# A new order of the first pair's front stages in a fused adapter-to-attention kernel

## The reference

```python
x = relu(x + df(x) * dt)                                   # L0: finite differences of x times five fixed grids
h = gelu(x @ down_W.T + down_b)                            # L1: adapter, 256 -> 64, with an expert per sequence
x = layernorm(x + (h @ expert_W[id].T + ...) @ up_W.T + up_b)
s, t = cond(time)                                          # L2: scale and shift from a small net on the time
y = silu(s * norm2d(x) + t) @ W_in + b_in                  #     norm2d: mean and variance over the whole 256 x 256
x = x + silu(s * norm2d(y) + t) @ W_out + b_out
x = ln(x) * (1 + scale) + shift                            # L3: scale and shift from a second embedding
q, k, v = x @ Wq + bq, x @ Wk + bk, x @ Wv + bv            #     16 heads of width 16
x = x + softmax(q k / 4 + attention_bias, masked) v @ Wo + bo
return x + (gelu2(ln(x) * g2 + beta2 @ W1 + b1) @ W2 + b2)
```

## Time and profile before

| what | value |
|---|---|
| median of three runs | 933.13 us (932.63 to 935.77) |
| span of the profiled execution | 929.6 us |
| median less that span | 3.5 us |
| PE busy | 856.0 us (92%) |
| DVE, ACT, POOL busy | 742.4, 727.5, 237.6 us |
| first product of q with k on record | at 92.17 us |

### The profile page before, as it was taken

One profiled execution on the slowest core, in us unless ns is written; L12 is line 12 of the kernel. 1 busy time (PEld: TensorE's weight loads), 2 busy tenths in 40 slices (PEclk: granted clock), 3 DMA queues, 4 the chain that ended last, 5 costly groups with the idle time before them and its releaser, 6 DMA issues.

```text
span 929.6 us, 18071 instructions
## 1 busy us (share of the span) xinstructions
PE 856.0 (92%) x5630; PEld 659.5 (71%) x5715; DVE 742.4 (80%) x2377; ACT 727.5 (78%) x1897; POOL 237.6 (26%) x236
## 2 busy tenths in 40 slices
PE   7775878999999999999999999999999999999987
PEld 6454656777777777777777777777777777777766
DVE  8556888898898898898898898898897898866542
ACT  1122978979898888979898888979898888988763
POOL 2232123224123323223123323223123323120000
PEclk9777899999999999999999999999999999999999
DMA  9813644554447363654447363554447363555400
GB/s 258 250 50 101 188 136 138 154 162 138 132 131 187 98 168 105 168 160 136 133 131 188 98 170 104 169 161 132 136 131 188 98 170 102 158 161 167 140 12 23
DMA packets 133081, 130.88 MB, mean 141 GB/s; under 512 B 18265, under 2 KB 123481, under 8 KB 132969
## 3 DMA queue, kind: packets, MB, share of 16 engines
q1 hardware_dynamic: 101616, 112.02, 42.9%
q10 hardware_dynamic: 31370, 17.71, 6.9%
HBM read 112.61 MB, written 17.07 MB: 140 GB/s over the span
## 4 chain that ended last, share of the span: by engine, by line
PE 58%; ACT 19%; DVE 7%; issue 3%; POOL 0%; ACTq 0%; DVEq 0%
PE ff_ps L1340 11%; PE ff_ps L1321 8%; PE PT_ps L1376 8%; ACT Pr L1073 5%; PE G L1144 5%; PE G L1136 5%; PE scores_ps L1361 4%; PE ctx_ps L1398 3%; ACT L1073 3%; DVE bias L931 2%; PE scores_ps L1358 2%; PE ff_ps L1307 2%; ACT tanh L1055 2%; ACT ffT L1059 2%; ACT PT L1086 2%
## 5 line engine op out<-in xcount | busy, mean ns | idle before, releaser
L1073 ACT ACTIVATE Pr<-bias,nmax 128x256 f32<-128x256 f32 x512 | 255.7, 506 | 35.0 <-DVE nmax L931 34.5
L931 DVE CUSTOM_DVE_ANT_0 bias<-scores_ps,bias 128x256 f32<-128x256 f32 x512 | 194.0, 420 | 48.1 <-PE scores_ps L1361 27.9
L1086 ACT ACTIVATE PT<-PT_ps 128x512 f32<-128x512 f32 x256 | 152.2, 595 | 51.8 <-PE PT_ps L1376 47.1
L1376 PE MATMUL PT_ps<-ident,Pr 128*128 128x128 f32 x1024 | 155.6, 274 | 8.0 <-ACT Pr L1073 8.0
L560 POOL TENSOR_TENSOR rstd<-var,half_neg 128x2 f32<-128x2 f32 (+1 forms) x64 | 43.2, 674 | 387.6 <-DVE var L684 252.4
L1376 PEld LDWEIGHTS PT_ps<-ident,Pr 128*128 128x128 f32 x1024 | 119.6, 140 | 16.8 <-ACT Pr L1073 13.2
L1321 PE MATMUL ff_ps<-ctxT,w 128*128 128x256 f32 x480 | 117.2, 387 | 12.8 <-ACT ffT L1059 10.7
L1340 PE MATMUL ff_ps<-w,ffT 128*128 128x256 f32 x480 | 113.1, 381 | 0.2 <-DVE ffT L908 0.2
L1321 PEld LDWEIGHTS ff_ps<-ctxT,w 128*128 128x128 f32 x480 | 86.3, 190 | 32.5 <-ACT ffT L1059 16.2
L1361 PE MATMUL scores_ps<-k_stack,q_stack 96*128 96x256 bf16 x512 | 98.7, 273 | 7.3 <-issue 2.1
L1073 ACT ACTIVATION_READ_ACCUMULATOR Pr<-bias,nmax 128x1 f32 x512 | 100.5, 196 | 0.0
(11 more groups left out here) (216 smaller groups left out, 1637.2 us busy)
## 6 DMA issues: line engine op xcount, KB each, us to landing
bias<-in_fside_Bx16xSxS_dram SPq DMA_DIRECT2D x256, 256.0 KB, 3.2
part_dram<-front ACTq DMA_DIRECT2D x32, 384.0 KB, 2.8
q_stack<-part_dram SPq DMA_DIRECT2D x32, 192.0 KB, 3.2
k_stack<-part_dram SPq DMA_DIRECT2D x32, 192.0 KB, 3.9
F<-in_x_dram SPq DMA_DIRECT2D x16, 256.0 KB, 3.7
ada<-rows_dram SPq DMA_DIRECT2D x16, 256.0 KB, 5.3
q_stack<-part_dram SPq DMA_DIRECT2D x32, 128.0 KB, 3.2
k_stack<-part_dram SPq DMA_DIRECT2D x32, 128.0 KB, 3.8
```

Source lines behind the costliest of these rows:

```text
L931: nc.vector.tensor_tensor_reduce(out=t, in0=SP_[:, n % 2, q * S:(q + 1) * S], in1=t, scale=-1.0, scalar=BIG, op0=ALU.add, op1=ALU.min, acc ...
L1073: ins = nc.scalar.activation(Pr[:, n % PR, q, :], bias[:, n // CH % RING, 2 * (n % CH) + q, :], ACT.Exp, bias=nmax[:, n, q:q + 1], scale=-1.0,
L1086: nc.scalar.activation(PT[:, m % BATCH, :, :].rearrange("p c q -> p (c q)"), TP[:, m % 2, :], ACT.Identity).then_inc(pt_ok, 1)
L1376: ins = pe.transpose(TP[:, m % 2, c * S + q * P:c * S + (q + 1) * P], Pr[:, m % PR, q, c * P:(c + 1) * P], ident[:, :])
```

## The change

Four edits, all of which concern pair 0 only, save the third:

1. New slots in `AT_FIRST`. The conditioning net moves ahead of `l0` of member 0; the front of member 1 (`diffs` to `x2`) moves forward, in between the steps of member 0; `inv3` of member 0 moves ahead of the masks on POOL.
2. The three copies of the conditioning net move from DVE to ACT. A Gelu of one element (`s_gelu`) is added on ACT behind the silu of `s_h1`.
3. `part_written` becomes one semaphore for q and one for k. SP loads q's parts when q is written and then waits for k. This holds for all pairs. On SP the transfers of the expert weights now stand ahead of those of the mask and of `w_in` and `w_out`.
4. For pair 0, member 0, k's product goes to the bank `ff_ps` and no longer waits for `qf`. And `WARM` has 41 products more, 49 where 8 were (six ahead of `s_h2`, into bank G; two each ahead of `down`, `expert` and `up`; 4 ahead of `avg0`; 10, before 8, ahead of `w_in`; 6 ahead of `w_out`; 14 ahead of `x3_turn`; 3 ahead of `q`).

Sums and values are the same in both kernels. The diff, cut:

```diff
-            "s_grid": (4.25, 4.25), "s_h1": (5.5, 5.5), "s_h2": (6.5, 6.5), "s_h2t": (6.75, 6.75), "s_sel": (2, 2),
+            "s_grid": (4.25, 4.25), "s_h1": (3, 3), "s_h2": (3.5, 3.5), "s_h2t": (3.75, 3.75), "s_sel": (2, 2),
...
-WARM = {"begin": 50, ("w_in", 0): 8}
+WARM = {"begin": 50, "s_h2": 6, ("down", 0): 2, ("expert", 0): 2, ("up", 0): 2, ("avg0", 0): 4, ("w_in", 0): 10,
+        ("w_out", 0): 6, ("x3_turn", 0): 14, ("q", 0): 3}
...
-        part_written = [sem(f"part_written{b}") for b in range(2)]
+        part_written = [[sem(f"{n}_written{b}") for b in range(2)] for n in "qk"]
...
+        def k_bank(j, b):
+
+            return Ft if j == 0 and b == 0 else GF[b]
...
-                if g == 0:
-                    wait_alone(sp, part_written[b], (j + 1) * 32)
                 for w, order in enumerate((Q_PLACE, K_PART)):
+                    if g == 0:
+                        wait_alone(sp, part_written[w][b], (j + 1) * 16)
                     for s, count in STACK_RUNS:
...
-                if once("s_h2", j, n):
-                    dve.wait_ge(h2_mm, 1)
-                    nc.vector.tensor_copy(h2_raw, FP[:, 0:P]).then_inc(h2_raw_ok, 1)
...
+                if once("s_h2", j, n):
+                    act.wait_ge(h2_mm, 1)
+                    evac(h2_raw, FP[:, 0:P], h2_raw_ok)
+                if once("s_h2t", j, n):
+                    act.wait_ge(h2_tr, 1)
+                    for m in range(4):
+                        evac(h2[:, m, 0:B], FP[:, P + m * TILE:P + m * TILE + B], h2_ok, b=cb2[:, m:m + 1])
+                if once("s_cond", j, n):
+                    act.wait_ge(cond_mm, 1)
+                    evac(cond_raw, SP_[:, 0, 0:2 * P], cond_raw_ok)
+                if once("s_gelu", j, n):
+                    act.wait_ge(const_set, 5)
+                    nc.scalar.activation(first_gelu[:, :], zero_eps[:, 0:1], ACT.Gelu)
...
-                            evac(qkf[w][b][:, c, :], GF[b][:, c, :], qk_ok[w] if c else None,
+                            evac(qkf[w][b][:, c, :], (GF[b], k_bank(j, b))[w][:, c, :], qk_ok[w] if c else None,
...
-            def warm(where):
+            def warm(where, bank=CP):
 
                 for _ in range(WARM.get(where, 0)):
-                    pe.matmul(CP[:, 0:P], mean_mat[:, :], mean_mat[:, :], start=True, stop=True)
...
+                    pe.matmul(bank[:, 0:P], mean_mat[:, :], mean_mat[:, :], start=True, stop=True)
...
                 for b in seqs("k", j, n):
+                    if not later(j):
+                        warm(("k", b))
+                    if k_bank(j, b) is not Ft:
+                        pe.wait_ge(qk_ok[0], 2 * j + b + 1)
+                    by_feature(wk, x4T[:, :, b * S:(b + 1) * S], k_bank(j, b)).then_inc(qkv_mm[1], 1)
+                for b in seqs("v", j, n):
+                    if not later(j):
+                        warm(("v", b))
                     pe.wait_ge(qk_ok[0], 2 * j + b + 1)
-                    by_feature(wk, x4T[:, :, b * S:(b + 1) * S], b).then_inc(qkv_mm[1], 1)
```

More of the change, by code:

```diff
@@ L88 @@
       "k_out": (28, 41.75), "v": (28.75, 46), "V": (29, 46.5), "mask": (20, 2)}
-AT_FIRST = {"s_sin": (0.25, 0.25), "s_se": (2.75, 2.75), "s_trig": (3.5, 3.5), "s_onehot": (4, 4),
-            "s_grid": (4.25, 4.25), "s_h1": (5.5, 5.5), "s_h2": (6.5, 6.5), "s_h2t": (6.75, 6.75), "s_sel": (2, 2),
-            "s_cond": (9.25, 9.25), "s_condt": (10.5, 10.5), "s_mask": (24.25, 24.25), "s_rows": (15.25, 15.25),
+AT_FIRST = {"s_gelu": (3.25, 3.25), "s_sin": (0.25, 0.25), "s_se": (2.75, 2.75), "s_trig": (3.5, 3.5), "s_onehot": (4, 4),
+            "s_grid": (4.25, 4.25), "s_h1": (3, 3), "s_h2": (3.5, 3.5), "s_h2t": (3.75, 3.75), "s_sel": (2, 2),
+            "s_cond": (4.5, 4.5), "s_condt": (6.25, 6.25), "s_mask": (24.25, 24.25), "s_rows": (15.25, 15.25),
             "x4": (28, 46.75), "s_fill": (4.25, 4.25), "s_bq": (7.75, 7.75), "s_w2": (34.25, 34.25),
-            "prods_p": (0.25, 7), "prods": (5.5, 6), "diffs": (5.5, 13), "edges": (5.5, 13.25), "l0": (3.25, 19.5),
-            "x1": (5.75, 18.25), "relu": (3, 11.5), "x1_turn": (3.75, 21), "x1T": (3.75, 13), "res1": (5.75, 21.75),
-            "down": (6.25, 21), "hid": (5.75, 17), "expert": (6.5, 22), "expT": (6.5, 19.5), "up": (8.5, 22),
[1 row of a table removed]
+            "prods_p": (0.25, 5.5), "prods": (5.5, 6), "diffs": (5.5, 6.5), "edges": (5.5, 6.5), "l0": (4, 8.75),
+            "x1": (5.75, 12), "relu": (4.25, 7), "x1_turn": (4.75, 16.5), "x1T": (5, 7.25), "res1": (5.75, 13.75),
+            "down": (6.25, 16.75), "hid": (5.75, 7.5), "expert": (6.5, 17.5), "expT": (6.5, 7.75), "up": (8.5, 18),
[1 row of a table added]
             "var0": (10.25, 24), "inv1": (10.75, 31.5), "x2_turn": (12, 25), "aff0": (11.75, 24.5),
             "x2b": (13.5, 34.5), "y0": (6.75, 30.5), "w_in": (16, 28.75), "z": (13.25, 27.5), "avg1": (17, 29.5),
[2 rows of a table removed]
[2 rows of a table added]
             "q": (22.5, 40), "qf": (28, 39.75), "q_split": (22.25, 40.25), "q_out": (28, 40.75), "k": (22.5, 40.75),
@@ L512, in _ @@
                 sp.dma_start(dst[:, :, :], mat(name)).then_inc(norm_loaded, 16)
[L513 to L517, removed]
             sp.wait_ge(sel_ok, 2)
@@ L525, in _ @@
                     sp.dma_start(ew[t * A:(t + 1) * A, seq, :], sel_in[:, seq, :]).then_inc(ew_loaded[part], 16)
+            load_mask(0)
+            for dst, name in ((w_in, "L2_cond_W_in"), (w_out, "L2_cond_W_out")):
+                sp.dma_start(dst[:, :, :], mat(name)).then_inc(film_loaded, 16)
+            sp.dma_start(b_in[:, :], i["L2_cond_b_in"]).then_inc(film_loaded, 16)
+            sp.dma_start(b_out[:, :], i["L2_cond_b_out"].partition_broadcast(P)).then_inc(film_loaded, 16)
             for dst, name in ((wq, "L3_cond_Wq"), (wk, "L3_cond_Wk"), (wv, "L3_cond_Wv")):
@@ L567, in front @@
                     if later(j):
-                        pool.wait_ge(part_written[b], j * 32)
+                        pool.wait_ge(part_written[0][b], j * 16)
+                        pool.wait_ge(part_written[1][b], j * 16)
                     else:
@@ L750, in front @@
                     dve.wait_ge(gB0_in, 16)
-                if once("s_h2", j, n):
-                    dve.wait_ge(h2_mm, 1)
-                    nc.vector.tensor_copy(h2_raw, FP[:, 0:P]).then_inc(h2_raw_ok, 1)
-                if once("s_h2t", j, n):
-                    dve.wait_ge(h2_tr, 1)
-                    for m in range(4):
-                        nc.vector.tensor_scalar(h2[:, m, 0:B], FP[:, P + m * TILE:P + m * TILE + B], cb2[:, m:m + 1], None,
-                                                ALU.add).then_inc(h2_ok, 1)
-                if once("s_cond", j, n):
-                    dve.wait_ge(cond_mm, 1)
-                    nc.vector.tensor_copy(cond_raw, SP_[:, 0, 0:2 * P]).then_inc(cond_raw_ok, 1)
                 if once("s_condt", j, n):
@@ L1225, in front @@
                 for b in seqs("x1_turn", j, n):
+                    if not later(j):
+                        warm(("x1_turn", b))
                     pe.wait_ge(x1_ok, 2 * j + b + 1)
@@ L1228, in front @@
                 for b in seqs("down", j, n):
+                    if not later(j):
+                        warm(("down", b))
                     pe.wait_ge(x1T_ok, 2 * j + b + 1)
@@ L1237, in front @@
                 for b in seqs("expert", j, n):
+                    if not later(j):
+                        warm(("expert", b))
                     pe.wait_ge(hid_ok, 2 * j + b + 1)
@@ L1244, in front @@
                 for b in seqs("up", j, n):
+                    if not later(j):
+                        warm(("up", b))
                     pe.wait_ge(expT_ok, 2 * j + b + 1)
@@ L1265, in front @@
                                 pe.wait_ge(film_loaded, 4 * 16)
-                            by_feature(w_in, yT[b], b).then_inc(win_mm, 1)
+                            by_feature(w_in, yT[b], GF[b]).then_inc(win_mm, 1)
                 for b in seqs("w_out", j, n):
+                    if not later(j):
+                        warm(("w_out", b))
                     pe.wait_ge(mstat_read[b], 2 * j + 2)
@@ L1282, in front @@
                         pe.wait_ge(qkv_loaded, 7 * 16)
-                    by_feature(wq, x4T[:, :, b * S:(b + 1) * S], b).then_inc(qkv_mm[0], 1)
+                    by_feature(wq, x4T[:, :, b * S:(b + 1) * S], GF[b]).then_inc(qkv_mm[0], 1)
                 for b in seqs("k", j, n):
+                    if not later(j):
+                        warm(("k", b))
[3 more added lines that the diff above has]
+                for b in seqs("v", j, n):
+                    if not later(j):
+                        warm(("v", b))
                     pe.wait_ge(qk_ok[0], 2 * j + b + 1)
-                    by_feature(wk, x4T[:, :, b * S:(b + 1) * S], b).then_inc(qkv_mm[1], 1)
-                for b in seqs("v", j, n):
-                    pe.wait_ge(qk_ok[1], 2 * j + b + 1)
+                    if k_bank(j, b) is not Ft:
```

(1 more changed line is left out.)

11 lines of the change are left out of this document (7 added, 4 removed), and 6 rows, old and new, of the table AT_FIRST.

## The result

The changed kernel takes 922.31 us (median of 4 runs, 921.24 to 927.10) beside 932.88 us (931.90 to 935.77) for the kernel before: a ratio of 0.9885, 95% interval 0.9861 to 0.9910, so 10.6 us, or 1.1%, faster. (The 933.13 us of the first table is the median of the three runs that stood when the forecast was made; a fourth, of 931.90, brings it to 932.88.) The profiled execution of the changed kernel took 923.14 us with a span of 921.1. The forecast was 924.0 us, a span of 920.5.

A forecast was written before the change was run, and what follows sets the result against it. TensorE was taken as nearly full behind a start of waiting engines. Steps to the first scores summed to 9.1 us earlier, making the 929.6 span 920.5; 3.5 more gave 924.0 us, range 920.5 to 929.5.

The forecast's parts named there:

- `x1`: Member 0's step behind `l0` on VectorE: starts at 27.4, 1.9 us earlier, with `l0` at full clock.
- `xs`: Member 0's step on VectorE: starts at 36.9 instead of 39.47, 2.6 us earlier, with one slow operation counted.
- the early Gelu: Gelu table loaded early on ScalarE: worth nothing, as 2.5 us of slack cover the 1.28 it takes away.
- `w_in`: Member 0's product on TensorE: starts at 48.4, 1.7 us earlier, its idle products late by about 0.9.
- `y1`: Member 0, behind a Silu table load and two activations on ScalarE: 57.8, against 58.6 before.
- From `y1` to the end of `w_out`: Member 0's `w_out` on TensorE: takes 2.3 us, with six idle products ahead of it, ending at 60.1.
- `xn3`: Member 0 on VectorE: near 63.4 as sign, 63.7 in the sum; masks behind `inv3` save some 1.6 us.
- the 14 products: Idle products ahead of member 0's `x3_turn` on TensorE: take 4.1 us, end at 64.2 and so decide.
- The gate behind `k_split`: From `k_split` to the first scores, through member 1's second mean: about 12.0 us, the last gate.
- From span to time: Whole kernel: median time stands 3.5 us above the span, so 920.5 becomes 924.0.
- its last two terms: About 12.0 us from `k_split` to the first scores, then an unchanged 837 us to the end.
- Rival (a): Full clock throughout the start: q done at 65.7, 11.2 us gained, time 921.9; chance 0.14.

The follow-up runs named there:

- the first experiment: The changed kernel with the idle products of the kernel before (50 at the start, 8 ahead of `w_in`): 928.41 us, ratio 0.9947.
- the order alone: The changed kernel with idle products as before, k's bank and q/k signals as before, and no early Gelu: 931.22 us, ratio 0.9976.

## Why the prediction was right, by its steps

The early steps came out as they were worked: `x1` 27.4 forecast, 27.43 measured; `xs` 36.9 and 36.73, with the one slow operation of 1.76 us on F (at 30.02) that the sum had counted; the early Gelu worth nothing; q at full clock; k's wait of 0.58 gone; the gate of the scores handed from the transfers to the second mean.

- **`w_in`: 48.4 forecast, 46.94 measured**, just below the 47 to 49 that the prediction gives as its sign. The mean came at 42.48 instead of 42.9, and the ten idle products took 2.40 us where the sum had 2.95, since the clock was back by then. They ended before `y0` was there; I had them 0.9 late.
- **`y1`: 57.8 and 55.85.** 1.5 of the 2.0 us came with `w_in`. The new wait is there, but small: the Silu load ends at 54.75, behind VectorE's result at 54.42, so it is 0.3 us. ScalarE after:

```profile
53.47 1.28 ACT L1031 ACT_TABLE_LOAD   x1
54.76 1.09 ACT L1031 ACTIVATE front<-front,cond 128x256 f32<-128x256 f32 x2
```

The Silu activation starts 0.01 us behind its load, and the Gelu (52.10) 0.02 us behind the load at 50.80. The drain that the Trainium skill gives beside the load ("ScalarE: Activation LUTs", section "What ACT_TABLE_LOAD costs") isn't seen in these rows either.

- **From `y1` to the end of `w_out`: 2.3 and 3.5.** The sum has `w_out` follow `y1` at once. The six idle products ahead of it ran at half clock (2.77 us) and held its start until 1.35 us behind `y1`, and `w_out` itself took 2.14 us. That took back 1.2 of the 2.0 us that `y1` was early. The products cost no more than they brought: at the 3.75 us of the first experiment `w_out` would have ended near 59.75 (an estimate: 55.85, the 0.15 that lie between the two in the first experiment, and 3.75), and it ended at 59.34.

- **`xn3`: 63.4 and 62.22.** (63.4 is the prediction's sign; its sum, 60.1 + 2.8, starts `xn3` at 62.9 and ends it at 63.7.) The time from `x3`, 2.8 us, was right, its cause wrong: I put the 1.6 us down to moving `inv3` ahead of the masks. The run with the masks first shows the same 2.9. What freed `inv3` is GpSimd's `res1` of member 1, before and after:

```profile
61.93 1.27 POOL L585 TENSOR_TENSOR front<-front,up_b 128x512 f32<-128x512 f32 x1 [6.02 <-ACT front L999]
```

```profile
47.95 1.27 POOL L592 TENSOR_TENSOR front<-front,up_b 128x512 f32<-128x512 f32 x1 [2.74 <-ACT front L1009]
```

Before, the masks ran right behind it; with it out of the way they are done by 61.3 in the run that has them first.

- **`x3_turn`: the 14 products do not decide.** I had them end at 64.2; they end at 62.5, and TensorE waits 0.94 us for VectorE.
- **The gate behind `k_split`: 12.0 and 12.35.** I had copied the 11.3 us of before; v took 3.62 instead of 2.88, the clock having fallen behind k. In the run without the early Gelu, with v at 1.89, the gate is 11.2.
- **Behind the scores: 837.4 and 838.4.** 1 us is given back.
- **From span to time: 3.5 and 2.0.** The runs of after have 2.0 to 2.1 us between span and time. So 1.5 of my 3.5 was that the profiled execution of before was a quick one, and not, as the text beside the first table has it, time around the program's instructions. The span was forecast at 920.5 and came at 921.1; the time was forecast at 924.0 and came at 922.31.

The forecast was 0.7 to 2.0 us late from `w_in` on and still 0.8 late at `k_split`, and its last two terms were too short by 0.35 and 1.0. That the span came out within 0.6 owes something to luck.

Rival (a), full clock throughout at 921.9, is closer to the median of 922.31 than the forecast is. In the traced execution it isn't what happened: the clock fell at `l0` of member 1, at `w_out` and behind k, and q was done at 67.16, between its 65.7 and the 67.8 of the forecast. But two other executions took 921.24 and 921.47, with a mean granted clock of 0.989 and 0.987 instead of 0.983, and they weren't traced; the run without the early Gelu (921.83 in its trace, clock 0.989) had `l0` of member 1 and v at full clock. So the forecast and (a) may each describe some executions of one kernel; that isn't shown. A fourth execution took 927.10, and nothing on record says why.

What the sum missed in kind is that the terms are not independent. The order alone is worth 2.4 us, the idle products and k's edits in the old order 0.6 as placed after (not clear of nothing), and all together 10.6. The order opens gaps ahead of `x3_turn`, `w_in` and `w_out` (4.06, 1.05 and 0.78 us in the first experiment), and only in a gap does an idle product cost nothing. Not tried: moving the second mean of member 1 behind the first scores, which is what they now wait for. Not taken apart: within "the order alone", the slots, the copies on ScalarE and SP's new order of transfers.

## What to carry to other kernels

An idle product is worth its clock only where the engine would have waited: read the wait ahead of the next real instruction first, and lay in no more than fits it, or reckon the excess against what the clock returns. Walk a forecast along the path step by step and name what ends last at each, but price the parts together: a change of order may bring little itself and yet make room for what does. Once another engine ends last, a higher clock brings little.

## What the runs showed of the hardware

The same queue doesn't always meet the same clock. Two kernels with the same work and the same pause (2.68 and 2.67 us) ahead of `l0` of member 1 ran it at different levels: the changed kernel, then the one with the masks first, windows of 1 us:

```profile
38.00:39.00 1.00, 1.00 (x4) 0.73 (x3) 0.86 (x5) 0.00 (x0) 0.17 (x1) 0.50 1.10 353
```

```profile
38.00:39.00 1.00, 1.00 (x9) 0.36 (x8) 0.96 (x5) 0.00 (x0) 0.51 (x1) 1.00 1.03 349
```

The granted clock is 0.50 in one and 1.00 in the other. And with k's edits undone, `x1` of member 0 waited 5.03 us for an `l0` at half clock, with the same six idle products ahead that gave 3.40 in the changed kernel. A single execution shows whether the clock can fall at a place, not that it does each time.
